# Two side groups in every seventh dense round of the count stage, none in the rounds behind the last build

## What is computed

```python
row, col = edge_index[0], edge_index[1]            # src, dst
deg = jnp.bincount(row, length=n).astype(x.dtype)
deg_inv_sqrt = jnp.where(deg > 0, rsqrt(deg), 0.0)
msg = (deg_inv_sqrt[row] * deg_inv_sqrt[col])[:, None] * x[col]
agg = jax.ops.segment_sum(msg, row, num_segments=n)
out = relu(agg @ W.T + b)
```

## Time and profile before

| | |
|---|---|
| median of 3 runs | 6223.08 us (6220.06 to 6224.97) |
| profiled execution, its own time | 6221.48 us |
| its span, first to last instruction | 6219.7 us |
| count stage, about | 505 to 2065 us of the span |
| busy TensorE / VectorE / ScalarE / POOL, share of the span | 83 / 58 / 27 / 65% |
| mean granted TensorE clock | 0.904 of 2.4 GHz |

### The profile page before, as it was taken

One profiled execution on the slowest core, in us unless ns is written; L12 is line 12 of the kernel. 1 busy time (PEld: TensorE's weight loads), 2 busy tenths in 40 slices (PEclk: granted clock), 3 DMA queues, 4 the chain that ended last, 5 costly groups with the idle time before them and its releaser, 6 DMA issues. The chain is left out here.

```text
span 6219.7 us, 151139 instructions
## 1 busy us (share of the span) xinstructions
PE 5132.7 (83%) x40344; PEld 4287.2 (69%) x40345; DVE 3576.8 (58%) x11440; ACT 1696.2 (27%) x3086; POOL 4071.6 (65%) x3911
## 2 busy tenths in 40 slices
PE   4885999999999668878887877878778888887877
PEld 3883899999998556666666666666666666666666
DVE  8998999999996543444443444444344434344444
ACT  3226666666663221111111111111111111111110
POOL 2005656655556567777777777777777777777776
PEclk9998999999999778888888888888888888888888
DMA  9206999999999643333333333333333333333333
GB/s 164 31 0 154 274 289 287 288 290 291 292 290 266 132 117 85 83 85 83 85 85 83 85 83 85 83 85 83 84 85 83 85 84 84 83 85 83 85 83 69
DMA packets 654468, 816.52 MB, mean 131 GB/s; under 512 B 426784, under 2 KB 471554, under 8 KB 653856
## 3 DMA queue, kind: packets, MB, share of 16 engines
q1 hardware_dynamic: 478737, 592.97, 32.5%
q0 software_dynamic: 175616, 222.16, 17.1%
HBM read 564.19 MB, written 250.47 MB: 131 GB/s over the span
## 5 line engine op out<-in xcount | busy, mean ns | idle before, releaser
L1638 POOL DMA_INDIRECT p_got<-p_tab,idx_d x3136 | 2966.5, 946 | 974.6 <-issue 894.1
L1624 ACT ACTIVATE h<-z,b_col 128x512 f32<-128x512 f32 x784 | 538.7, 687 | 3402.2 <-PE z L1764 3329.8
L1628 DVE TENSOR_TENSOR h<-z,nb 128x512 f32<-128x512 f32 x784 | 541.9, 691 | 1595.6 <-PE z L1604 1591.7
L1598 PEld LDWEIGHTS z<-ident_f,p_got 128*128 128x128 f32 x3136 | 422.0, 162 | 1367.8 <-DMA p_got<-p_tab,idx_d 1212.7
L1598 PE MATMUL z<-ident_f,p_got 128*128 128x128 f32 x3136 | 602.0, 324 | 768.1 <-DMA p_got<-p_tab,idx_d 767.8
L837 POOL DMA_INDIRECT sum_tab<-val_s,idx_s x496 | 779.0, 1570 | 578.0 <-ACT val_s L949 454.1
L987 PE MATMUL a_ps<-tile_r,pair_l 128*128 128x288 fp8e5 x5280 | 1040.8, 286 | 72.6 <-DVE tile_r L1076 45.8
L1008 PE MATMUL out_ps<-gw,a_got 121*128 121x144 bf16 x11340 | 1079.9, 225 | 6.6 <-DMA a_got<-a_tab 6.5
L1604 PEld LDWEIGHTS z<-w_sb,h 128*128 128x128 f32 x6272 | 1043.0, 236 | 57.7
L1604 PE MATMUL z<-w_sb,h 128*128 128x128 f32 x6272 | 1032.0, 319 | 0.0
L958 ACT CAST stage<-a_ps 128x576 uint16<-128x576 f32 x1320 | 837.1, 639 | 422.2 <-PE a_ps L987 417.3
(11 more groups left out here) (201 smaller groups left out, 3702.8 us busy)
## 6 DMA issues: line engine op xcount, KB each, us to landing
a_tab<-stage SPq DMA_DIRECT2D x330, 576.0 KB
a_got<-a_tab SPq DMA_DIRECT2D x330, 576.0 KB
rel<-rel_row SPq DMA_DIRECT2D x392, 192.0 KB
p_got<-p_tab,idx_d POOLq DMA_INDIRECT x3136
ef<-in_edge_t SPq DMA_DIRECT2D x392, 64.0 KB
q_win<-q_tab SPq DMA_DIRECT2D x784, 24.0 KB
src_bc<-src_row SPq DMA_DIRECT2D x124, 128.0 KB
a_tab<-big SPq DMA_DIRECT2D x22, 472.5 KB
```

The lines of the kernel that those rows point to most:

```text
L1598: pe.matmul(out_tile, p_rows[:, j, :], ident_f[:, :], start=False, stop=False, is_transpose=True, skip_group_check=True)
L1638: pool.indirect_dma_start(p_rows[:, j, :], None, p_tab, bass.IndirectOffsetOnAxis(idx[:, j:j + 1], 0)).then_inc(landed, 16)
```

## The change

Groups are no longer tied to rounds one to one. `sides(r)` lists the groups of round r: rounds 13, 20, 27, ... 104 (14 of them, `two_sides`) have two, the other rounds up to 109 one, and the rounds from 110 on none, so that all 124 groups are done in the 110 rounds that build. `placed` gives each group of a round its shift: 0 where it is alone, and -3 and +2 windows (twice as many turns on TensorE) where there are two. VectorE's side steps now stand behind the adds of the same window, where they stood ahead of them. SyncE in a double round with groups f and f+1 loads behind stage 0 the source row and the feature rows of f+1, behind stage 1 the source row of f+2 and behind stage 2 its feature rows. The single group behind the sweeps is gone on every engine. `sweep` makes its loops of rounds that are alike in this too, so that more of them stand as code of their own, and ScalarE's single loop becomes one per stretch between double rounds.

```diff
+    MORE_EACH = 7
+    two_sides = range(LAG, ROUNDS, MORE_EACH)
+    assert len(two_sides) == SG - ROUNDS and two_sides[-1] < ROUNDS
+    def sides(r):
+        first = len([x for x in two_sides if x < r])
+        return () if r >= ROUNDS else (first, first + 1) if r in two_sides else (first,)
...
+                EARLY, LATE = -3, 2
...
+                def placed(r, side):
+                    shifts = (EARLY, LATE) if len(side) == 2 else (0,)
+                    return [(r + o, w) for o, w in zip(side, shifts)]
...
-                    for r in range(SG):
+                    for r in range(ROUNDS):
...
-                        scatter(r)
+                        for e, _ in placed(r, sides(r)):
+                            scatter(e)
...
-                    def body(r, u, seg, n, sb_index, home, tail=0):
-                        following = r + 1 if isinstance(r, int) else sp.snap(r + 1)
+                    def body(r, u, seg, n, sb_index, home, side, tail=0):
+                        after = [following(e) for e, _ in placed(r, side)]
                         for k in range(GROUPS):
                             if READ * k < n:
                                 save(r, k, home)
                             if u is not None:
                                 load(u, seg, k, sb_index)
-                            if k == 0:
-                                load_src(following)
-                            if k == 1:
-                                load_g(following)
+                            if len(after) == 2 and k < 2:
+                                load_src(after[k])
+                                if k == 0:
+                                    load_g(after[0])
+                            elif len(after) == 2:
+                                load_g(after[1])
+                            elif after and after[0] is not None and k < 2:
+                                (load_src, load_g)[k](after[0])
...
-                            if i == MIX_KEPT_AT:
-                                keep_mix(r)
-                            if i == VAL_KEPT_AT:
-                                keep_val(r, s)
+                            for k, (e, shift) in enumerate(placed(r, side)):
+                                if i == MIX_KEPT_AT + shift:
+                                    keep_mix(e)
+                                if i == VAL_KEPT_AT + shift:
+                                    keep_val(e, (s + k) % 2)
...
-                            if turn_of == MIX_AT:
-                                mix_rows(r)
-                            if turn_of == SUM_AT:
-                                sum_rows(r)
+                            for e, shift in placed(r, side):
+                                if turn_of == MIX_AT + 2 * shift:
+                                    mix_rows(e)
+                                if turn_of == SUM_AT + 2 * shift:
+                                    sum_rows(e)
...
-                    for e in range(ROUNDS + LAG, SG):
-                        mix_rows(e)
-                        sum_rows(e)
...
-                            if i == PICK_AT:
-                                pick_same(r)
-                            if i == MOVE_AT:
-                                move_same(r)
-                            if i == NUMBER_AT:
-                                number(r)
                             if i in ADD_AT and u is not None:
                                 add_out(u, seg, ADD_AT.index(i), sb_index > 0, tail)
+                            for e, shift in placed(r, side):
+                                if i == PICK_AT + shift:
+                                    pick_same(e)
+                                if i == MOVE_AT + shift:
+                                    move_same(e)
+                                if i == NUMBER_AT + shift:
+                                    number(e)
```

More of the change, by code:

```diff
@@ L90, in lagged, with sweep @@
         body(k, k % 2)
-def sweep(eng, windows, lag, body):
+def sweep(eng, windows, lag, sides, body):
     units = -(-windows // (ROUND * FOLD)) * FOLD
@@ L101, in like @@
     def like(r):
[L102 to L118, removed]
-            if hi - lo == 1:
-                body(u + lo + lag, u + lo, lo, n, sb, home)
-            elif n == 0 and lo == 1 and sb == units // FOLD - 1:
+        home = (built(r), r // FOLD) if built(r) else (0, -1)
+        return home + ((r - lag) // FOLD if r >= lag else -1, sides(r), built(r + 1) > 0)
+    lo = 0
+    while lo < units + lag:
+        starts = lo == 0 or lo >= lag and (lo - lag) % FOLD == 0
+        hi = lo + 1
+        while not starts and hi < units + lag and like(hi) == like(lo) and (hi < lag or (hi - lag) % FOLD):
+            hi += 1
+        n, home, sb, side, _ = like(lo)
+        home = max(home, 0)
+        if sb < 0:
+            if hi - lo == 1:
+                body(lo, None, None, n, 0, home, side)
+            else:
+                with eng.Fori(lo, hi) as r:
+                    body(r, None, None, n, 0, home, side)
+        else:
+            u = sb * FOLD
+            at = lo - lag - u
+            if hi - lo == 1:
+                body(lo, lo - lag, at, n, sb, home, side)
+            elif n == 0 and at == 1 and hi == units + lag:
                 with eng.Fori(0, (hi - lo) // 2) as t:
@@ L124, in sweep @@
                         k = eng.snap(t * 2 + (2 - other))
-                        body(eng.snap(k + (u + lag)), eng.snap(k + u), k, n, sb, home, 1 + other)
+                        body(eng.snap(k + (u + lag)), eng.snap(k + u), k, n, sb, home, side, 1 + other)
             else:
-                with eng.Fori(lo, hi) as k:
-                    body(eng.snap(k + (u + lag)), eng.snap(k + u), k, n, sb, home)
-            lo = hi
+                with eng.Fori(at, at + hi - lo) as k:
+                    body(eng.snap(k + (u + lag)), eng.snap(k + u), k, n, sb, home, side)
+        lo = hi
 def in_slot(q, slot, slots, per):
@@ L856, in _ @@
                     SCAN_FROM = 2 * LAG
-                    assert due(NS - 1, ROUND - 1) < SG and SCAN_FROM + 3 * SCANS < SG
-                    for r in range(SG):
+                    assert due(NS - 1, ROUND - 1) < ROUNDS and SCAN_FROM + 3 * SCANS < SG
+                    for r in range(ROUNDS):
                         if r >= SCAN_FROM and (r - SCAN_FROM) % 3 == 0 and (r - SCAN_FROM) // 3 < SCANS:
@@ L900, in load_g, with following @@
                                      ).then_inc(g_win_loaded, 16)
-                    def body(r, u, seg, n, sb_index, home, tail=0):
-                        following = r + 1 if isinstance(r, int) else sp.snap(r + 1)
+                    def following(e):
+                        return None if isinstance(e, int) and e + 1 == SG else e + 1 if isinstance(e, int) else sp.snap(e + 1)
+                    def body(r, u, seg, n, sb_index, home, side, tail=0):
+                        after = [following(e) for e, _ in placed(r, side)]
                         for k in range(GROUPS):
@@ L949, in keep_val, with body @@
                         act.copy(val_s[s][:, :, :].rearrange("p j f -> p (j f)"), sum_ps).then_inc(val_ready, 1)
-                    def body(r, s):
+                    def body(r, side, s):
                         for i in range(ROUND):
@@ L959, in body @@
                                      a_ps[:, 2 * (i % 2):2 * (i % 2) + 2, 0:PIECE]).then_inc(kept, 1)
-                            if i == MIX_KEPT_AT:
-                                keep_mix(r)
-                            if i == VAL_KEPT_AT:
-                                keep_val(r, s)
[L965 to L972, removed]
+                            for k, (e, shift) in enumerate(placed(r, side)):
[3 more added lines that the diff above has]
+                                    keep_val(e, (s + k) % 2)
+                    r = 0
+                    while r < ROUNDS:
+                        side = sides(r)
+                        s = (r + side[0]) % 2
+                        pairs = 0
+                        while r > 0 and r + 2 * pairs + 1 < ROUNDS and sides(r + 2 * pairs) == sides(r + 2 * pairs + 1) == side:
+                            pairs += 1
+                        if pairs > 1:
+                            with act.Fori(0, pairs) as t:
+                                for o in range(2):
+                                    body(act.snap(t * 2 + (r + o)), side, (s + o) % 2)
+                            r += 2 * pairs
+                        else:
+                            body(r, side, s)
+                            r += 1
                 @block.tensor
@@ L1049, in body @@
                                         unit(u, seg, rows + k % READ, bank, sb_index, tail)
-                    sweep(pe, DW, LAG, body)
-                    for e in range(ROUNDS + LAG, SG):
-                        mix_rows(e)
-                        sum_rows(e)
+                    sweep(pe, DW, LAG, sides, body)
                 @block.vector
```

(2 more changed lines are left out.)

5 lines of the change are left out of this document (1 added, 4 removed).

## The result

The kernel with the change takes 6289.5 us, median of 4 executions (6288.6 to 6291.2), against 6223.7 of the kernel before (6220.1 to 6225.0): **1.0106 times as long [1.0093, 1.0118]**, slower by 65.8 us. The profiled execution's span is 6288.0 us, before 6219.7: 68.3 more.

A forecast was written before the change was run, and what follows sets the result against it. TensorE, without gaps in dense rounds, was taken as the bound; 14 x (0.43 + 3.74 + 1.53) = +79.8 us, less 30.6 behind the last build, gives +49.2: 6272 us, own range 6255 to 6285, wider 6221 to 6296.

The forecast's parts named there:

- Faster: Rival on double rounds: the second group's row lands as if alone, under about 2.7 us; 6210 us, chance 0.14.
- No difference: Rival: only the stage-0 save and load precede the row, landing 3.4 us after issue, clock kept; 6223 us, chance 0.12.
- Worse: Rival: DMA is the bound, landings grow to 5.94 us and tail loads come no sooner; 6294 us, chance 0.12.
- TensorE's stall: Double rounds: TensorE waits for the tile behind the late source row, 3.74 us each, 14 times; bounds 0.9 to 4.3.
- The landing: Double rounds: the second group's source row lands 5.4 us after its issue, at 1906.7.
- the row's issue stays where it is: Double rounds: the earlier first pick does not move the second row's issue, since the save still waits for four kept windows.
- The clock: Behind each double-round stall: TensorE's halved clock costs 1.53 us, 14 times; bounds 0 and 1.53.
- The early half: First group of a double round: its mix and sum are not late, their row and g_win_s requested a round before.
- I put nothing on the following rounds: Rounds after a double one: VectorE, 92.6 busy of 100, regains its lead, so no cost was added.
- Behind the last build: Stretch after the builds: side work removed, rounds 111 to 122 at 7.0 us, shorter end; -30.6 us, bounds -16.3 and -32.5.
- change of stage: End of the stage: 4.4 us, 2060.9 to 2065.31, taken to remain after the change, behind VectorE's last add of 1.0.
- keep_val ... no wait: Double rounds: the second group's keep_val needs scatters issued a round earlier, landing in at most 5.5 us; no wait.

The follow-up runs named there:

- e1: Changed kernel, but in double rounds the second group's source row is requested ahead of the stage-0 save and load, without the save's wait; 6220.5 us, 0.9985 of the kernel before.
- e2: Changed kernel, but in double rounds the second group's row goes ahead of the stage-0 save and load, keeping the save's wait; 6231.5 us, 1.0003 of the kernel before.
- e9: Changed kernel with first group's shift -2 and a second row buffer filled one round ahead, behind stage 1; 6211.5 us, 0.9967 of the kernel before.
- e3: Changed kernel plus 14 filler matmuls on TensorE in each double round's stall; 6271.3 us, 1.0065 of the kernel before.
- e5: Changed kernel with the first group's shift -2 instead of -3; 6285.0 us, 1.0104 of the kernel before.
- e4: Changed kernel with side groups 110 to 123 left out, so no round is double; 6203.5 us, 0.9956 of the kernel before.
- e7: Changed kernel with shift -2 and a second row buffer, filled at the head of the double round; 6208.8 us, 0.9981 of the kernel before.
- e6: Changed kernel with the second group's row ahead of the stage-0 save and load, and first group's shift -2; 6215.1 us, 0.9992 of the kernel before.
- e8: Changed kernel with shift -2 and a second row buffer filled one round ahead, on a slower chip; 7159.2 us, 1.0007 of the kernel before there.

## Why the prediction was right, point by point

**The cause and its sign held.** It named the one buffer, the row's issue behind save and load of stage 0, VectorE waiting at hot_s, TensorE behind it, and the clock. e1 and e2 show that the stall and the clock hang on the row's place and time alone. The total was less exact: 6289.5 us lies above the forecast's own range, 6255 to 6285, and inside the wider one, 6221 to 6296, that takes in two rivals. *Faster* fell: the row took 5.9 us, where it needed under 2.7; even in e2, first of its round, it took 4.4. The estimate of 2.3 us by the Trainium skill (DMA: Bandwidth & Descriptors, Anatomy of one DMA) rests on a fit for one DMA on GpSimd's path; this row goes by SyncE's queue. The trace has one row with little else in flight, the first of the count stage in the kernel before, and it took 3.1 us:

```profile
512.83 0.35 SPq L893 DMA_DIRECT2D src_bc<-src_row  x1
...
515.95 0.36 DVE L1110 TENSOR_TENSOR hot_s<-rows_s,key_l 128x384 bf16<-128x384 bf16 x1 [4.98 <-DMA src_bc<-src_row]
...
512.83:515.95 3.12, 0.58 (x4) 0.26 (x4) 0.00 (x1) 0.96 (x2) 0.00 (x0) 0.89 0.35 79
```

So no row of these runs comes under the 2.7 that *faster* wanted. *No difference* fell by the same rows, for it wanted 3.4 (its own figures, 1280 KB at 291 GB/s from 1899.92, give 3.1). *Worse* fell with the DMA share of 0.94 and with e1, where the share is 0.99 and the loss is gone.

| step | predicted, us | measured, us |
|---|---|---|
| added matmuls, 14 x 0.43 | 6.0 | at most 8.1 (e9, whole dense part) |
| row to landing | 5.4 | 5.94 |
| VectorE's wait | 4.9 | 4.81 |
| the tile of window 4, 14 times | 0 | 0.34 |
| TensorE's stall, 14 times | 3.74 | 3.67 idle, 3.83 from start to start |
| the clock, 14 times | 1.53 | 1.95 (e3) |
| behind the stall, other than the clock, 14 times | 0 | 0.11 (e3) |
| following rounds | 0 | 1.1 in all |
| dense part | +79.8 | +95.0 |
| units of rounds 110 to 122 | -14.6 | -8.9 |
| the end | -16.0 | -20.1 |
| all | +49.2 | +66.0 to the next stage, +65.8 median |

**The landing** was 0.5 us longer than put, and the wait and the stall still right: VectorE came to hot_s 1.1 us behind the issue and not 0.5, and TensorE ran dry 4.6 us behind it and not 3.6. In part that is because "the row's issue stays where it is" does not hold: it comes 1.59 us behind the first build of window 4, in the kernel before 2.23 us. Two errors cancelled; that the stall was met to 0.1 us is luck.

**The clock** is the first term mis-sized: "I add 1.53 per double round" came from one row behind an idle of 1.97 us. After stands of 3.1 to 4.4 us TensorE worked 3.2 to 5.9 us at half clock, which cost 1.95 us in the mean. That makes 5.9 us of the 15.2 missing.

**The early half** is the second. "The early mix and sum of f are not late" looked at their loads alone. They were not late for a load, but the early pick makes the tile of window 4 late: 0.34 us each, 4.8 us (e5).

**"I put nothing on the following rounds"** held: by the build starts all rounds between the double ones together lose 1.1 us, so the lead that VectorE lost costs next to nothing later. The terms close: 14 x (0.43 + 0.34 + 3.83 + 1.95 + 0.11) = 93.2, with the 1.1 and 0.7 that stand ahead of the first double round 95.0.

**Behind the last build** the total was close, 28.9 for 30.6, by two errors against each other. Units 111 on were put at 7.0 us and took 7.59, since a load takes 4.95 us there and not 4.0: with scatters and rows gone the landing shrank by a tenth, not by a quarter. The end was put at 5.4 us behind the last unit and took 1.3. The step that failed is the 4.4 us "change of stage". In the kernel before, the last scatter had landed at 2059.7, and 5.0 of the 5.6 us from there to 2065.3 are a drain, an instruction that POOL runs at the end of its block. First the kernel before, then the changed one (one line of the kernel asked for; length in ns, then the start):

```profile
L760 POOLq DRAIN  x1: 4963/4963/4963, 2060.0 to 2060.0; - x1
```

```profile
L770 POOLq DRAIN  x1: 2881/2881/2881, 2041.1 to 2041.1; - x1
```

With no scatter left by then POOL drains 90 us before the stage ends, beside TensorE's work, and only 1.3 us are left behind the last matmul (in e4 too, where the drain takes 4963 ns at 1944.2).

**Other engines.** POOL did not hold anything up, as predicted. "keep_val ... no wait" was wrong in the letter: ScalarE waits for scatters 93 times, 41.0 us in all, but 101 times and 51.1 us in the kernel before too. POOL alone waits for what it keeps, and POOL holds nobody up.

## What to carry to other kernels

When work is doubled up in a step, follow each of its loads through its queue: a small load issued behind two large ones took 5.9 us here, as long as they, and moving its use forward does nothing if its issue is tied to something else. Ask for it in the step before, into a buffer of its own, and look in the trace how far ahead that is (7 us here, for a landing of 6); both parts are needed: the buffer alone (e7) ended the dense part 2.3 us sooner than the mere new order (e6), and asking a round ahead (e9) another 8. Before pricing a stall of TensorE, add what the clock costs behind it, and look at the work that is moved forward too, and not only at its loads. Before giving a fixed cost to a change of stage, look which engine's instruction fills it and whether that will still be the last.

## What the runs showed of the hardware

- The same 128 KB took 5.94 us from issue to use behind a save and a load of 576 KB each, 4.39 ahead of them (e2), 5.9 behind the pair of the stage before (e7), and 3.1 with the DMA engines 35% busy (512.83 in the kernel before).
- A stand of 3.57 us brought the clock to 0.50 before it was over, and TensorE then worked 5.4 us at half speed. After another, of 3.69 us at 767.09, the clock was 0.50 from 768 to 771 and 0.97 in the next microsecond. Nearly equal stands, unequal prices: 2.4 and 1.6 us; over the 14 it is 1.3 to 1.6 us in seven and 1.9 to 2.7 in the other seven, where the half clock lasted twice as long. In e5 the first build pair behind a stand of 3.83 us still took its usual 0.41 us, and the next two 0.68. With the fillers of e3 the clock stayed at 1.00.
- The length of a stand alone does not tell: in e2 stands of up to 2.05 us left the clock at 1.00, and behind the 1.97 us that ended at 1941.91 in the kernel before it was 0.50.
- POOL's drain at the end of its block took 4.96 us in the kernel before and in e4, 2.88 us in the change and in e9, each 0.3 us behind the landing of its last scatter. What makes the difference was not found.
- One chip ran the kernel before in 7151.8 us. The granted clock in slices of the span, here from e8, is 7 tenths in the edge network, where the others have 8; whether that is all of the difference was not found.

```profile
PEclk9989999999997777777787777777777777777778
```
